# Bias products on full rows: 64 and 16 rows padded with zeros to 128 and 125 in an audio tower with switch routing

## The reference

```python
logits = xf @ switch_w.T + switch_b
routes = jnp.argmax(probs, axis=-1)
pos = <place of the token among those of its expert>
keep = pos < capacity                      # capacity = int(1.2 * 3000 / 16) = 225
buf = zeros((E, capacity, D)).at[routes, pos].set(xf)
y = jnp.einsum('ecd,efd->ecf', buf, expert_w) + expert_b[:, None, :]
out = jnp.where(keep[:, None], gathered, xf) * route_probs[:, None]
```

## Time and profile before

| | us |
|---|---|
| median of 3 runs | 431.52 |
| the profiled execution | 430.47 |
| its span, first to last instruction | 428.6 |
| PE busy / DVE busy / ACT busy / POOL busy | 398.0 / 345.3 / 216.6 / 149.9 |
| mean granted PE clock | 0.982 of full |

### The profile page before, as it was taken

One profiled execution on the slowest core, in us unless ns is written; L12 is line 12 of the kernel. 1 busy time (PEld: TensorE's weight loads), 2 busy tenths in 40 slices (PEclk: granted clock), 3 DMA queues, 4 the chain that ended last, 5 costly groups with the idle time before them and its releaser, 6 DMA issues.

```text
span 428.6 us, 7510 instructions
## 1 busy us (share of the span) xinstructions
PE 398.0 (93%) x2463; PEld 348.8 (81%) x2463; DVE 345.3 (81%) x930; ACT 216.6 (51%) x428; POOL 149.9 (35%) x197
## 2 busy tenths in 40 slices
PE   3898899999999999999999999999999686999893
PEld 2686788998899889888988898889888674889893
DVE  4547858968998899889988998899889974686786
ACT  3626428742874287428742874287428422761000
POOL 5101030122057205630563056305631551005872
PEclk9999999999999999999999999999999898999889
DMA  6374030001000100010001000100000027132135
GB/s 190 87 215 162 3 91 0 2 2 43 2 1 20 43 2 0 21 43 0 2 19 44 0 2 20 42 2 2 21 0 1 2 65 139 46 93 66 34 73 130
DMA packets 21076, 18.49 MB, mean 43 GB/s; under 512 B 5010, under 2 KB 17656, under 8 KB 20734
## 3 DMA queue, kind: packets, MB, share of 16 engines
q1 hardware_dynamic: 17054, 15.23, 13.4%
q0 software_dynamic: 2880, 2.35, 2.4%
q10 hardware_dynamic: 1104, 0.44, 0.5%
HBM read 11.33 MB, written 6.62 MB: 42 GB/s over the span
## 4 chain that ended last, share of the span: by engine, by line
PE 73%; DVE 7%; issue 6%; ACT 6%; DMA 4%; POOL 3%; ACTq 0%; SPq 0%; DVEq 0%; POOLq 0%
PE psB L946 10%; PE psB L947 10%; PE psB L948 10%; PE psC L972 7%; PE psC L1063 4%; PE psC L909 4%; PE psC L910 4%; PE psC L911 4%; PE psC L1080 4%; ACT h L641 2%; PE psC L1049 2%; DMA h2b<-slot_x 2%; PE psA L909 2%; ACT kT L628 1%; POOL h L600 1%
## 5 line engine op out<-in xcount | busy, mean ns | idle before, releaser
L946 PE MATMUL psB<-W2h,h1l 128*125 128x512 f32 x192 | 78.5, 409 | 0.1
L948 PE MATMUL psB<-W2h,h1h 128*125 128x512 f32 x192 | 75.8, 395 | 0.0
L947 PE MATMUL psB<-W2l,h1h 128*125 128x512 f32 x192 | 75.7, 394 | 0.0
L652 ACT ACTIVATE h2b<-h2b 125x512 f32<-125x512 f32 x48 | 30.0, 627 | 48.2 <-DVE h2b L1409 48.1
L641 ACT ACTIVATE h<-psA,b1c 128x376 f32<-128x376 f32 x64 | 35.6, 576 | 19.9 <-PE psA L911 19.9
L1409 DVE TENSOR_TENSOR h2b<-psB,b2r 125x512 f32<-125x512 f32 x48 | 33.0, 688 | 14.4 <-PE psB L948 14.1
L948 PEld LDWEIGHTS psB<-W2h,h1h 128*125 128x125 f32 x192 | 35.5, 185 | 8.9
L946 PEld LDWEIGHTS psB<-W2h,h1l 128*125 128x125 f32 x192 | 35.7, 186 | 7.8 <-DVE h1l L1400 0.8
L947 PEld LDWEIGHTS psB<-W2l,h1h 128*125 128x125 f32 x192 | 35.7, 186 | 7.1
L1400 DVE TENSOR_TENSOR h1l<-h,h1h 128x1504 fp32r<-128x1504 f32 x16 | 27.6, 1728 | 13.3 <-ACT h1h L628 13.3
L517 POOL TENSOR_TENSOR sg<-euler,sg 125x6 f32<-125x6 f32 x8 | 10.7, 1334 | 73.3 <-DVE sg L1423 73.3
(11 more groups left out here) (266 smaller groups left out, 999.6 us busy)
## 6 DMA issues: line engine op xcount, KB each, us to landing
xt<-in_x SPq DMA_DIRECT2D x8, 336.0 KB
slot_x<-eb_parts SPq DMA_DIRECT2D x2, 960.0 KB, 8.5
basef<-in_L_tok_W SPq DMA_DIRECT2D x1, 1024.0 KB, 7.3
ewf<-slot_x SPq DMA_DIRECT2D x2, 480.0 KB, 6.4
h2b<-slot_x SPq DMA_DIRECT2D x2, 480.0 KB, 8.0
slot_y<-h SPq DMA_DIRECT2D x4, 240.0 KB, 2.5
slot_y<-A SPq DMA_DIRECT2D x4, 240.0 KB, 3.1
qa<-in_L_attn_w_qkv SPq DMA_DIRECT2D x1, 768.0 KB
```

What stands on the lines that cost most here:

```text
L652: nc.scalar.activation(slot, slot, ACT.Gelu).then_inc(c_g2.sem, 1)
L946: mm(ps, lo, W2h[:, k, :], start=k == 0, stop=False)
L947: mm(ps, hi, W2l[:, k, :], start=False, stop=False)
L948: last = mm(ps, hi, W2h[:, k, :], start=False, stop=k == HK - 1)
```

## The change

The 64-row product of each slot pair gets all 128 partitions of `eb_parts`, whose upper 64 are still zeros, and `part32` gets 128 partitions. The 16-row products of `dense_bias` get 125: `ebs` grows to 125 partitions, is zeroed by a memset on POOL and then loaded into its first 16; `ohT` and `rank_e` (16 minus the partition's number, so never a valid choice from partition 16 on) grow to 125. The new memset stands ahead of that of `xs` and counts on `s_zero`, so the waits on it go up by one. `ohT` of row 6 lies in `neg_g` and that of row 7 in `kT`, as before, only on more partitions.

```diff
-        rank_e = sb("rank_e", [E, 1])
+        rank_e = sb("rank_e", [TP, 1])
...
-        part32 = sb("part32", [64, TS], F32R)
-        ebs = sb("ebs", [E, C])
+        part32 = sb("part32", [128, TS], F32R)
+        ebs = sb("ebs", [TP, C])
...
-        ohT = {PRIOR: neg_g[0:E, :], LAST: kT[0:E, 0, 0:G]}
+        ohT = {PRIOR: neg_g[:], LAST: kT[0:TP, 0, 0:G]}
...
-            sp.wait_ge(s_zero, 1)
+            sp.wait_ge(s_zero, 2)
...
-                             (ebs[:], expert_b), (swf[:], switch_w), (swbr[:], switch_b.partition_broadcast(TP)),
+                             (ebs[0:E], expert_b), (swf[:], switch_w), (swbr[:], switch_b.partition_broadcast(TP)),
...
-            sp.wait_ge(s_zero, 2)
+            sp.wait_ge(s_zero, 3)
...
+            pool.memset(ebs[:], 0.0).then_inc(s_zero, 1)
             pool.memset(xs[:, 0, :], 0.0).then_inc(s_zero, 1)
...
-                bias = eb_parts[0:64, 2 * p * C:2 * (p + 1) * C].unsqueeze(1).to_broadcast([64, 2, 2 * C])
+                bias = eb_parts[:, 2 * p * C:2 * (p + 1) * C].unsqueeze(1).to_broadcast([128, 2, 2 * C])
...
-                vec.tensor_scalar(part32[:], ones[0:64, 0:TS], 1.0 / 32, None, ALU.mult).then_inc(s_ebl, 1)
+                vec.tensor_scalar(part32[:], ones[:, 0:TS], 1.0 / 32, None, ALU.mult).then_inc(s_ebl, 1)
...
-                vec.tensor_scalar(ohT[b], bank_chosen(b)[0:E, 0:G], rank_e[:, 0:1], None, ALU.is_equal).then_inc(s_only[b], 1)
+                vec.tensor_scalar(ohT[b], bank_chosen(b)[0:TP, 0:G], rank_e[:, 0:1], None, ALU.is_equal).then_inc(s_only[b], 1)
```

## The result

The changed kernel takes 429.04 us (median of ten runs, 427.36 to 430.7) against 431.86 for the kernel before (ten runs, 430.32 to 433.29): a ratio of 0.9932, 95% interval 0.9909 to 0.9954. That is about 2.9 us less, 2.0 to 3.9 by the interval. Measured again on another chip, beside other kernels, the ratio was 0.9896 (0.9861 to 0.9931). The forecast was 428.9, 2.6 less.

The account below looks back on a forecast made before the run. PE was taken to set the pace through all eight slot-expert steps. Product 0 (0.28) and products 1 to 6 (2.28) sum to 2.56, so 431.5 - 2.6 = 428.9 us, range 426.7 to 431.2.

Parts of the forecast that it names:

- 0.38 a product: Slot bias products on PE: full rows save 0.19 on the product and 0.19 on the pair of passes behind it.
- 2.28 for six: Slot products 1 to 6, at full clock ahead of L1174: 6 x 0.38 = 2.28 us saved.
- 0.28 for product 0: First slot product, in a half-clock stretch: 0.56 saved there, worth 0.28 us if the stretch ends when it did.
- The 2.56 of the sum: PE up to L1174: products 0 to 6 together make L1174 start 2.56 us earlier.
- The cover of 0.2: Ahead of L1174: DVE's `pp` would end at 379.51, L1174 could start at 379.71, so 0.2 us is to spare.
- Handed on by POOL: From L1174 through store, POOL's gathers and norms to the last row: everything moves by the same 2.56 us.
- The other edits: `ebs` memset costs 0.20 us, hidden before SP asks for `xs` at 3.01; wider mask L1708 costs nothing extra.
- The end: End of the kernel comes 2.56 us earlier, with the low stretch again and DVE's last row end at 423.0.
- rival 3: Half-clock stretch at 403 to 410 goes away, gaining 1.4 us at most beyond the sum: 427.5; chance 0.12.
- Rival 2: Clock stays low through the last row's dense steps, 12 us becoming 18: +3.0 us, 434.5; chance 0.04.
- Dense rows worth nothing: Both `dense_bias` savings of 0.38 us are off the path, lost beside POOL's gathers and DVE's masks.

Follow-up runs that it names:

- experiments 3 to 6: Against the kernel before: slot bias products on 96 rows (0.9965); all pair products on 64 (1.0083); bias products split in two on 64 (1.0139) or 128 rows (0.9944).
- the second profile: Another profile of the changed kernel, nothing altered, taken when it was measured again against the kernel before: 428.68 us, ratio 0.9896.
- experiment 4: Kernel before with each pair's four expert products also on 64 rows, leaving out half the channels: 435.11 us, ratio 1.0083.
- the next move in the same place: Changed kernel with pair 7's products ahead of row 6's transposes, its copies ahead of the masks; against the kernel before 428.63 us (0.9925), then 428.2 (0.9895).
- experiment 5: Kernel before with each slot pair's 64-row bias product split into two of 256 columns, without the repeated operand: 437.86 us, ratio 1.0139.
- the repeat of 4: The kernel with all pair products on 64 rows, unchanged, run again for a second profile of the clock: 434.38 us.

## Why the prediction was right

- **0.38 a product.** Right: 0.42 to 0.23 and 0.41 to 0.22, and shown by experiments 3 to 6 to belong to the change of row count. From pair 1 in the chain (362.81, now 363.45) to L1174's piece (382.43, now 380.83) it is 19.62 against 17.38, 2.24 less; forecast 2.28 for six.
- **0.28 for product 0.** Not what this profile shows: up to pair 1 the stretch shrank from 5.38 to 4.55, 0.83. I let the half-clock stretch end when it did before. It was as long (3.4), but began at 358.7, ahead of the first transpose, where before it began at 359.0, 1.5 behind it; so it lay more over waiting and ended before product 0's pair was done. That is the place of the stretch in that execution, not the change. In the second profile it was 6.8 long and took the rest back: from the first transpose to L1175 it is 380.14 - 356.87 = 23.27, so 1.57 less than before and not 3.07. The 2.56 of the sum lies between the two.
- **The cover of 0.2.** Right: `pp` ended at 380.45, L1175 started at 380.67, without idle time ahead of it.

```profile
380.25 0.20 DVE L1641 TENSOR_TENSOR pp<-psA,oh 125x48 f32<-125x48 f32 x1
```

- **Handed on by POOL.** Right to 0.1 in every stretch.
- **The other edits.** Right: the memset of `ebs` moves that of `xs` from 1.56 to 1.70, and SP still asks for `xs` at 3.01; the mask L1709 takes 0.61 in the chain on 125 partitions for 0.60 on 16.
- **The end.** Here the steps differ from the forecast, without changing the number. In the first profile the half-clock stretch near 403 was 3.4 instead of 6.8 long, rival 3 in part, so that DVE's last string came sooner; and the last gather landed 5.0 after its start, not the 3.03 that I had taken from a scatter. The cap that I set for rival 3 was thus looser than the real one: the 1.4 was not there, and DVE waited. In the second profile the stretch was 6.8 long, as I had let it be, and the end was DVE's.
- **Rival 2.** No run had the low clock through the last row's dense steps. That the 12 us there would become 18 isn't worked out from a row shown, and no run shows it.
- **Dense rows worth nothing.** Not settled: PE saves the 0.38, and alone they gave 0.3 (interval from 1.4 faster to 0.7 slower). But the kernel with both parts measured 1.6 and 2.2 below the one with the slots alone, and the forecast has no place for that.

The measured 2.9 is above 2.6, within the interval. What is shown is the mechanism, and 1.6 to 3.1 of gain in the stretch up to L1175, by where the half-clock stretch lay. That the whole came within 0.3 of the forecast is in part luck: the forecast puts all 2.6 on the slots, and these alone measured 1.3 and 2.3.

## What to carry to other kernels

Where a PE stream sets the pace and a short product with few contraction rows stands between full ones, look at the pieces of the chain for it and for the product behind it, and at the loader's idle time "on issue" ahead of both; if they exceed those of full-row neighbours, pad the rows with zeros. Here a change of row count cost 0.19 us at full clock, with 512 columns as with 256, and 96 rows were already enough to avoid it. Narrow products side by side also change the row count only once, but the one kernel that had them (experiment 4) was 3.6 us slower, with a longer half-clock stretch. Before adding up such gains, follow them to the end of the kernel, and compare them with what a measurement can tell: the next move in the same place bought 0.6 us locally, which intervals of 2 us and a landing that varied by 1.9 don't let one see in the whole.

## What the runs showed of the hardware

- With more narrow products the clock came back later. With more of them behind the idle time at 357 us (experiments 4, 5 and the repeat of 4), TensorE stayed at 1.2 GHz for 13.6 or 13.7 us, in three profiles of three; with 96 or 128 rows it was 3.4 or 6.8, and 3.4 and 6.8 with the narrow bias products alone. At half clock over 6.8 to 10.3 us more, 3.4 to 5.1 are lost (an estimate: half of that time), which fits the 3.6 of experiment 4 and the unexplained 3 of experiment 5. That the row count itself does it is the likeliest reading, argued and not shown.
- A weight load whose product uses 64 or 16 rows isn't done under a running product on full rows, nor a full one under these. Eight 64-row products left the loader idle for 1.9 us ahead of them and 2.1 behind; on 128 rows it was 0.1 and 0.6. Behind the 16-row products the load of the first L1195 starts with its product, at 388.54; behind those on 125 rows it starts 0.10 ahead of it, 386.19 for 386.29. The Trainium skill says in "TensorEngine Tiling (Array Packing)", Key Properties, that changing the tiling mode drains the engine; the 0.19 at each change agrees. The Trainium skill's rule in "TensorE: Matmul & The Clock Gate", Part 3, that loads overlap running products only where the row group differs, doesn't hold here: 32 full-row loads (L1164) behind full-row products had 0.0 us of idle time.
- The load of the slots took between 6.09 and 7.95 us from its issue, and the last gather 4.06 to 5.99 from its start, in profiles of kernels that don't differ there. Such landings and the length of the half-clock stretches can make up much of the spread of 3 us between runs of one kernel; no run tells their shares apart.
